# First attention layer: products read PSUM, the aggregate is no longer copied, VectorE's slots are dealt out anew

## The reference

```python
queries, gates = (qg[..., :DIM_KEYS], qg[..., DIM_KEYS:])
keys, values = (kv[..., :DIM_KEYS], kv[..., DIM_KEYS:])
queries, keys, values = (l2norm(queries), l2norm(keys), l2norm(values))
sim = jnp.einsum('bhid,bhjd->bhij', queries, keys)
attn = jnp.square(jax.nn.relu(sim))
aggr = jnp.einsum('bhij,bhjd->bhid', attn, values)
out = tanh_norm(aggr) * jnp.tanh(jax.nn.silu(gates))
return out.transpose(0, 2, 1, 3).reshape(b, n, h * d) @ Wout
```

## Time and profile before

| | us |
|---|---|
| median of 3 runs | 1835.48 |
| lowest, highest | 1835.18, 1840.15 |
| the profiled execution | 1857.31 |
| its span | 1854.6 |
| PE busy in the span | 1273.5 (69%) |
| DVE busy | 1229.5 (66%) |
| POOL busy | 926.3 (50%) |
| ACT busy | 740.7 (40%) |

### The profile page before, as it was taken

How to read it: one execution, slowest core, us unless ns; L and a number is a source line. 1 busy time by engine, 2 the same in 40 slices (tenths; PEclk the granted TensorE clock), 3 DMA queues, 4 the chain that set the end, 5 groups by cost and what they waited for, 6 DMA issues and landing times.

```text
span 1854.6 us, 27625 instructions
## 1 busy us (share of the span) xinstructions
PE 1273.5 (69%) x8554; PEld 857.2 (46%) x8555; DVE 1229.5 (66%) x2820; ACT 740.7 (40%) x1207; POOL 926.3 (50%) x996
## 2 busy tenths in 40 slices
PE   2434332548888887878788887568778777783775
PEld 1222221425666666656566667523333333331665
DVE  6778771157788887777777784266777677663443
ACT  1101100335455554455445544145555555552322
POOL 2355566546666666666666644321332313223663
PEclk8555555568888888888988886669988898986988
DMA  4000002600000000000000000030000000000110
GB/s 130 25 16 26 14 2 52 132 12 2 7 8 8 7 6 3 3 6 6 6 6 6 7 4 4 16 104 13 18 10 17 9 17 17 9 12 21 60 58 13
DMA packets 73493, 41.41 MB, mean 22 GB/s; under 512 B 23825, under 2 KB 68729, under 8 KB 73424
## 3 DMA queue, kind: packets, MB, share of 16 engines
q1 hardware_dynamic: 53040, 28.88, 5.6%
q0 software_dynamic: 20384, 11.67, 3.1%
HBM read 31.63 MB, written 23.87 MB: 30 GB/s over the span
## 4 chain that ended last, share of the span: by engine, by line
PE 40%; DVE 33%; issue 10%; ACT 6%; POOL 5%; DMA 2%; another core or an unknown queue 1%; POOLq 1%; DVEq 0%; SPq 0%; ACTq 0%
PE psum L1111 8%; PE psum L1162 5%; PE psum L1216 4%; DVE terms L1731 4%; DVE o L1573 4%; PE psum L1345 2%; PE psum L1358 2%; POOL o_inv L634 2%; PE psum L1139 2%; PE psum L1239 2%; PE psum L1249 2%; PE psum L1277 2%; PE psum L1120 1%; DVE rden L1425 1%; POOL xe_dram L573 1%
## 5 line engine op out<-in xcount | busy, mean ns | idle before, releaser
L1111 PE MATMUL psum<-v,attn 128*128 128x64 f32 x2048 | 288.5, 301 | 25.7 <-ACT aggr L845 17.1
L1111 PEld LDWEIGHTS psum<-v,attn 128*128 128x128 f32 x2048 | 272.7, 214 | 61.6 <-issue 44.9
L1731 DVE TENSOR_REDUCE terms<-psum 128x2 bf16<-128x512 f32 x256 | 165.5, 690 | 37.2 <-PE psum L1239 28.5
L609 POOL DMA_INDIRECT yg<-ye_dram,routel x128 | 139.2, 1088 | 65.5 <-issue 36.0
L695 POOL TENSOR_SCALAR veps<-meanvar 128x2 f32<-128x2 f32 x32 | 6.1, 191 | 330.9 <-DVE meanvar L1709 329.8
L573 POOL DMA_INDIRECT xe_dram<-rows_out,route x128 | 131.1, 1024 | 39.6 <-issue 38.7
L1216 PE MATMUL psum<-prob,v 128*32 128x256 f32 x1024 | 148.8, 415 | 1.1 <-ACT pvT L919 0.8
L914 ACT ACTIVATE prob<-psum 128x512 f32<-128x512 f32 x256 | 138.5, 597 | 18.8 <-PE psum L1204 18.8
L830 ACT ACTIVATE attn<-psum 128x1024 f32<-128x1024 f32 x128 | 129.9, 1015 | 11.9 <-PE psum L1094 10.7
L1120 PE MATMUL psum<-ident,o 128*128 128x128 f32 x256 | 48.5, 351 | 102.3 <-DVE o L1573 78.9
L1239 PE MATMUL psum<-k_highT,q_highT 32*128 32x256 bf16 x512 | 56.6, 303 | 76.9 <-DVE terms L1731 73.0
(11 more groups left out here) (297 smaller groups left out, 2975.8 us busy)
## 6 DMA issues: line engine op xcount, KB each, us to landing
x4n_dram<-x4n SPq DMA_DIRECT2D x16, 256.0 KB
w<-in_w POOLq DMA_DIRECT2D x48, 64.0 KB, 2.5
x_in<-in_x SPq DMA_DIRECT2D x8, 256.0 KB, 2.8
xe_dram<-zero_rows SPq DMA_DIRECT2D x8, 256.0 KB, 3.5
x_dram<-x1s SPq DMA_DIRECT2D x8, 256.0 KB
xe_dram<-rows_out,route POOLq DMA_INDIRECT x128
xe<-xe_dram SPq DMA_DIRECT2D x16, 128.0 KB
x1l<-x_dram SPq DMA_DIRECT2D x16, 128.0 KB, 2.2
```

The lines of the kernel that those rows point to most:

```text
L609: pool.indirect_dma_start(yg[p][:, j, k, :], None, ye_dram, bass.IndirectOffsetOnAxis(ap=where[:, j, K0 + k:K0 + k + 1], axis=0), bounds_c ...
L1111: mm = pe.matmul(psum[:, 4 + j, (head % HALF) * DV:(head % HALF + 1) * DV], attn[g % RING][:, h, c * SEQ + j * P:c * SEQ + (j + 1) * P], v ...
L1731: dve.tensor_reduce(terms4[:, 0, j, head:head + 2, 6, 0], bank[4 + a2].rearrange("q (b k) -> q b k", b=2), AX, ALU.max, negate=True).then_ ...
```

## The change

1. The aggregate is not copied. ACT squares banks 4 and 5 straight from PSUM in two pieces of 512 columns, and DVE multiplies the same banks with the unscaled gate (`product_with_gate`), also in two pieces, into `o`, of which there are now two tiles. ACT takes bank 4 first, DVE bank 5 first, then each waits for the other to be done with the second bank. PE may fill the banks again when both pieces of both engines are done.
2. POOL scales the product `o` with `o_factor` (`scale_output`) in place of the gate. There is no DVE instruction behind it: PE transposes each piece as soon as it is scaled.
3. The squares of the attention: DVE multiplies the relu in SBUF with the scores still in PSUM, now for six pairs; ACT squares pairs 2 and 4 in SBUF (`ACT_PAIRS`); POOL squares none. PE's `scores` of pair `g` waits for the square of pair `g-2` where DVE makes it.
4. On DVE, the product comes right behind the square in slots 1 and 5, `norm_of(tail, 1)` moves from slot 1 to the end of slot 2, the terms are split behind the product and the norm of slot 5, and combine is cut: two experts' rows in slot 4, two with the moments in slot 6; `normalise3` moves to slot 7.
5. On POOL, `length_of(att, 0)` comes behind `rstd3` instead of ahead of it.
6. On ACT, the first gate tanh moves from slot 5 to slot 4.

```diff
-        aggr = sb("aggr", [P, 2, 512])
-        o = sb("o", [P, 2, 512])
+        o = two("o", [P, 2, 512])
...
-        POOL_PAIRS = (2, 3, 6)
+        ACT_PAIRS = (2, 4)
+        DVE_PAIRS = tuple(g for g in range(PAIRS) if g not in ACT_PAIRS)
...
             def half(fetch, front, att, tail):
...
                 if tail:
                     length_of(tail, 1)
-                if att:
-                    square(att, POOL_PAIRS[0])
-                if tail:
-                    scale_gate(tail, 1)
-                if att:
-                    square(att, POOL_PAIRS[1])
+                    scale_output(tail, 1)
...
-                if att:
-                    length_of(att, 0)
                 if fetch:
                     hold(s["var3"], fetch.n)
...
                 if att:
-                    scale_gate(att, 0)
-                if att:
-                    square(att, POOL_PAIRS[2])
+                    length_of(att, 0)
+                    scale_output(att, 0)
...
             def take_aggregate(q, hf):
-                wait(act, s["o_made"], 2 * (q.n - 1) + hf)
+                wait(act, s["o_norm_made"], 2 * (q.n - 1) + hf)
                 act.wait_ge(s["attn_read"], PAIRS * (q.n - 1) + 4 * hf + 4)
-                act.activation(aggr[:], psum[:, 4:6, :], ACT.Copy).then_inc(s["aggr_out"], 1)
-                act.wait_ge(s["aggr_out"], 2 * (q.n - 1) + hf + 1)
-                act.activation(aggr_sq[:], aggr[:], ACT.Square).then_inc(s["aggr_sq_made"], 1)
+                act.activation(aggr_sq[:, 0, :], psum[:, 4, :], ACT.Square).then_inc(s["aggr_sq_made"], 1)
+                act.wait_ge(s["o_product"], 4 * (q.n - 1) + 2 * hf + 1)
+                act.activation(aggr_sq[:, 1, :], psum[:, 5, :], ACT.Square).then_inc(s["aggr_sq_made"], 1)
...
+                    if att and g in ACT_PAIRS:
+                        square(att, g)
+                    if front and g == 4:
+                        gate_tanh(front, 0)
...
             def scores(att, g):
-                wait(pe, s["relu_made"], PAIRS * (att.n - 1) + g - 1)
+                before, n = (g - 2) % PAIRS, att.n - 1 - (g < 2)
+                if before in ACT_PAIRS:
+                    wait(pe, s["relu_made"], PAIRS * n + before + 1)
+                else:
+                    wait(pe, s["attn_made"], len(DVE_PAIRS) * n + DVE_PAIRS.index(before) + 1)
...
                 if g % 4 == 0:
-                    wait(pe, s["aggr_out"], 2 * (q.n - 1) + hf)
+                    wait(pe, s["aggr_sq_made"], 4 * (q.n - 1) + 2 * hf)
+                    wait(pe, s["o_product"], 4 * (q.n - 1) + 2 * hf)
...
-                dve.tensor_tensor(r[:], r[:], r[:], ALU.mult).then_inc(s["attn_made"], 1)
+                dve.tensor_tensor(r[:], r[:], psum[:, 2 * (g % 2):2 * (g % 2) + 2, :], ALU.mult).then_inc(s["attn_made"], 1)
...
-            def gated_output(q, hf):
-                wait(dve, s["oT_ps"], 4 * (q.n - 1) + 2 * hf)
-                dve.wait_ge(s["gated"], 4 * (q.n - 1) + 2 * hf + 2)
-                dve.tensor_tensor(o[:], aggr[:], gate[q.p][:, :, 512 * hf:512 * hf + 512], ALU.mult).then_inc(s["o_made"], 1)
+            def product_with_gate(q, hf):
+                wait(dve, s["oT_ps"], 4 * (q.n - 2) + 2 * hf + 2)
+                dve.wait_ge(s["gate_made"], 2 * q.n)
+                dve.wait_ge(s["attn_read"], PAIRS * (q.n - 1) + 4 * hf + 4)
+                for j in (1, 0):
+                    if j == 0:
+                        dve.wait_ge(s["aggr_sq_made"], 4 * (q.n - 1) + 2 * hf + 1)
+                    dve.tensor_tensor(o[hf][:, j, :], psum[:, 4 + j, :], gate[q.p][:, j, 512 * hf:512 * hf + 512], ALU.mult).then_inc(s["o_product"], 1)
```

More of the change, by code:

```diff
@@ L837, in gate_tanh @@
             def gate_tanh(front, j):
[L838 removed]
+                wait(act, s["o_product"], 4 * (front.n - 2))
                 act.wait_ge(s["silu_made"], 4 * (front.n - 1) + 2 * j + 2)
@@ L887, in half @@
                         take_oT(tail, 1)
-                    if front and g == 5:
-                        gate_tanh(front, 0)
                     if att and g == 5:
@@ L1577, in take_oT, with combine @@
                 dve.tensor_copy(oT[:, 1, 4 * hf:4 * hf + 4, :], ring[OT_BANK[hf][1]][:].rearrange("q (c t) -> q c t", c=4)).then_inc(s["oT_dve"], 1)
-            def combine(front):
-                dve.wait_ge(s["x1l_landed"][front.p], 16 * front.k)
-                dve.wait_ge(s["yg_landed"][front.p], 16 * 2 * K0 * front.k)
-                for k in range(K0):
+            def combine(front, part):
+                if part == 0:
+                    dve.wait_ge(s["x1l_landed"][front.p], 16 * front.k)
+                    dve.wait_ge(s["yg_landed"][front.p], 16 * 2 * K0 * front.k)
+                for k in range(2 * part, 2 * part + 2):
                     for j in range(2):
@@ L1629, in half @@
                         square(tail, PAIRS - 1)
-                    if g > 0 and att and g - 1 not in POOL_PAIRS:
+                    if g > 0 and att and g - 1 in DVE_PAIRS:
                         square(att, g - 1)
@@ L1658, in half @@
                         v_sum(front, 3)
-                    if tail and g == 4:
-                        gated_output(tail, 1)
                     if front and g == 3:
```

62 lines of the change are left out of this document (33 added, 29 removed).

## The result

The changed kernel takes 1933.01 us (median of 4 runs, 1930.25 to 1944.54), the kernel before 1837.82 us (4 runs, 1835.18 to 1840.95). The ratio is 1.053, with a 95% interval from 1.048 to 1.058: 95 us slower. The forecast was 1917 us, with a range of 1868 to 1978.

A forecast was written before the change was run, and what follows sets the result against it. No engine is full; a 48 us step is PE work, low clock and idle. Per step -4.84 + 1.1 + 4.4 + 0.8 + 4.5 = +6.0 us, times 13.5 is 81 us: 1917 us, range 1868 to 1978.

The forecast's parts named there:

- The product leaves its place: DVE's gated product before the transposes of half 1: PE's wait of 4.84 us per step goes; pieces take 0.68 us.
- First cost: Turning of half 0: product pieces ahead of the value copies raise PE idle from 1.12 to about 2.2 us: +1.1.
- Second cost: Slot 2: ACT blocked at the tanh by the later norm; PE waits for the square of pair 2: +4.4.
- Third cost: Freeing the aggregate's banks: second pieces wait for the other engine's first, 2.0 us where one copy took 1.23: +0.8.
- Fourth cost: POOL's length of half 0 behind combine: PE's idle at the step's end goes from about 0.8 to 5.3 us: +4.5.
- The clock: PE's clock falls after the 4.4 us wait, losing 4.5 us as before at another place: net 0.
- rival B: PE's clock falls twice a step, each further fall 4.5 us: up to 1978 us, 1947 in half the steps; chance 0.20.
- Hidden: the multiply-adds: Combine's first part beside POOL's scaling of the values: multiply-adds taken as not held up, nothing charged.
- C: PE's clock stays up at the 4.4 us wait, saving about 3 us per step: 1876 us; chance 0.13.
- E: Effects cancel: second cost as reckoned, POOL's length early enough, no clock fall: about -20 to +20 us, 1835; chance 0.05.
- D: ACT reaches square of pair 2 within 4.3 us, neither stall nor clock fall: -8.2 per step, 1725 us; chance 0.06.

The follow-up runs named there:

- handover version: Changed kernel with norm in slot 1, length ahead of `rstd3`, DVE's slot 1 product behind the copies of values, ACT's slot 5 squares ahead of `oT`: 1762.27 us, 0.961.

## Why the prediction was right, and where it was not

**Direction and size.** Right. The profiled executions differ by 77 us, the sum said 81; the medians differ by 95. The 21.8 us by which the profiled execution of before lies over its median were carried over, and after's was not so far off its own: three of before's 13 steps are 50.5 to 51.1 us long and one 52.7, the others near 48, which is what I had taken as the step. Against that 48.0 the mean of after, 55.6, is +7.6 a step where +6.0 was forecast; against before's own mean of 49.0 it is +6.6. In 13.5 steps that makes 103 and 89 us, on either side of the 95 of the medians. So a step grew by 1 us or so more than forecast, and the terms make it up differently: that they sum to nearly the forecast is in part luck, as the terms below show.

**The product leaves its place (-4.84).** Confirmed. The wait is gone, the pieces take 0.69 us (0.68 by the earlier trace rows) and the squares from PSUM 1.21. Beside POOL's values stands a square, not the product as I had said: that begins 1.5 us after POOL is done (873.82, 867.95 + 4.40). It is the square that shows that an operand in PSUM keeps DVE clear of POOL.

**First cost (+1.1).** Confirmed to a tenth: 1.12 us became 2.16. With the product behind the copies it went back to 1.19.

**Second cost (+4.4).** Confirmed in place, releaser and mechanism: 4.0 us on average, 4.2 at most, with ACT in front of the tanh for 11.6 us (the 9 to 10 forecast was too short). What I had not seen is that PE's idle is not what makes up its price. Filling the idle with work that keeps the clock up, which leaves the wait, gave 15 us. Moving the tanh gave 88, more than that and the 54 us that 13.5 such waits contain. The tanh holds ACT, and behind ACT it holds DVE's inverse roots and with them all of the rest of the step. I had written that these stand behind the tanh, and then added up only PE's side of it.

**Third cost (+0.8).** Mechanism right, size wrong: 2.6 us on average where I took 2.0, before 1.23. ACT's first square (875.75) stands behind its copy `oT`, and DVE's second piece waits 1.88 us for it. That is +1.4 in place of +0.8.

**Fourth cost (+4.5).** The weakest term. The wait of ACT for the length came as forecast (10.43 us, forecast 10) and the second term transposes do wait for `qT`, but 2.45 us at most and 1.1 on average, not 2.9; the wait for `x3` of 0.9 did not appear; the last is 1.35 where 1.5 was reckoned. Together 2.5 against 5.3, so +1.7 in place of +4.5. The reckoning set PE's arrival with all rows at full clock. With a slower projection (5.30 us where I took 4.1), PE comes later and waits less. The run without this cost took 2.0 us off a step, near the 1.7.

**The clock (0).** Wrong, and the step of the forecast that failed; this is the part of rival B that came true. I had reckoned with one fall that only changes its place. In 5 of 13 steps there is another behind the longer idle in front of half 0's turning, in 11 of 13 the aggregate of pair 4 is slow again behind its wait (as it was in all 13 before, but there with the one fall at half 1's turning), and in 8 of 11 the queries' and keys' matmuls are slow behind the two waits that the fourth cost brings (in none of 13 before, and in none of 12 with the length first). By the stretches from 470 to 1090 us idle has grown by 2.7 a step (11.5 against 8.85; the terms above make 3.3), and PE's busy time, with the same matmuls, by 4.0 (44.1 against 40.1). The forecast had +6.0 and 0. So its sum was nearly right with much of the share turned round, and that is luck. Not all of the further low clock is on the path: the filling shows that most of what lies behind pair 2 is not.

**Hidden: the multiply-adds.** They are held, against my reading of the trace, and the rule that I set against it holds for POOL's long instructions. The Trainium skill (SBUF — State Buffer, "Who interferes with whom", practical consequences) says that a VectorE instruction with two SBUF inputs contends with a GpSimd instruction that reads SBUF. Beside POOL's scaling of the values this case agrees for multiply-adds (2.84 us for two, 0.35 each when moved), for squares (4.64) and for the scaling (4.00), and none with an operand in PSUM was held. The row that I took as counter-evidence had two multiply-adds beside `o_max` with 16 columns, which lasts 0.25 us and begins 0.27 us after them: there was nothing to wait for. But the six behind them do run beside POOL without being held. In the kernel before, 84 multiply-adds and 18 squares out of SBUF began while POOL's `o_inv` of 16 columns was under way, and took 0.34 to 0.35 us and 1.19 to 1.22 us each. So two SBUF inputs alone do not decide here; it matters which instruction POOL is at.

```profile
636.19 1.91 DVE L1586 SCALAR_TENSOR_TENSOR x<-yg,routel,x 128x128 f32<-128x128 f32 x6
```

```profile
636.15 2.93 POOL L634 TENSOR_TENSOR o_inv<-o_max,minus_half 128x16 f32<-128x16 f32 x1
```

The charge of nothing was right for the changed kernel, as the prediction says for both cases.

**What the sum left out.** In the kernel before, DVE's first three instructions of the inverse roots run beside POOL's scaling of the gate and its square. They have one SBUF input each and are held too: 0.65, 0.90 and 1.62 us on average from 470 to 1100 us. In the changed kernel POOL has no square there, and they take 0.92, 0.21 and 0.21. That shortens the chain from the tanh to the scores of pair 5 by 1.8 us a step, a gain that the sum has no term for. One of them in the kernel before, while POOL squares from 619.14 to 621.03:

```profile
619.28 1.82 DVE L1546 TENSOR_SCALAR inv<-guess 128x96 uint32<-128x96 uint32 x1
```

**The other rivals.** C (clock stays up) and E (cancel) are out by the low rows and the 2.4 us waits at the end. D is out for the changed kernel, but its condition, a tanh that comes 4.5 us earlier, is what the norm in slot 1 makes true: its single price of 1725 us was too good, since that run gives 1865, and with the length in its old place 1800.

## What to carry to other kernels

Before a small instruction is moved back in one engine's list, look for the wait that it feeds on another engine, and list everything that stands behind that wait: the price is that of the whole queue and of the engines fed by it, not the idle of the busiest engine in front of the first piece. The places of a norm (1.21 us) and a length (three POOL instructions, 3.4 us), both feeding a tanh of 0.22 us, decided here between +5.3% and -2.2%, with the heavy part of the change the same.

When two engines share out a buffer crosswise, put each one's first half ahead of any copy that nobody waits for yet; and when DVE works out of SBUF with two inputs, begin it before POOL's long operation and not behind it, or give it an operand in PSUM. The advice on the buffer rests on two moves that were made together (37 us), the advice on DVE and POOL on single edits (15 and 75 us).

## What the runs showed of the chip

**A short idle may or may not lower the clock.** In front of half 0's turning PE stood 1.11 to 1.20 us in each of 13 steps of the handover version and of the four built on it, and in 9 of 13 steps of the kernel before. The aggregate behind it took 2.0 us in all of those 74 cases. The four longer idles of the kernel before were followed by 3.67 us once (3.14 us of idle) and by 2.0 three times (2.58, 2.91 and 3.19). With 2.08 to 2.17 us of idle at the same place, in the same 13 steps, it took 3.2 to 3.7 us in 5 steps of the changed kernel, in 11 with the norm in slot 1, in 10 with the length first, in 8 with 16 matmuls put in, in 7 with the tanh in slot 4 and in 7 with norm and length, in 1 with the squares from SBUF and in none with 26 matmuls put in. And a shorter idle can do at another place: behind 1.63 to 1.76 us in front of the scores of pair 5, the turning of half 1 took 1.85 to 1.92 us in place of 1.04 in 9 of 13 steps of the handover version. So the length of the idle alone does not decide; what else does, no run here isolates.

**POOL is held up as well.** POOL's inverse root of 128x16 takes 2.94 us when nothing holds it (717.90 in the run with the square first); when DVE's terms with both inputs in SBUF had begun just ahead, it took 3.98. In the same step, POOL and the DVE row at that moment:

```profile
736.72 3.98 POOL L628 TENSOR_TENSOR o_inv<-o_max,minus_half 128x16 f32<-128x16 f32 x1
```

```profile
736.71 1.22 DVE L1624 TENSOR_TENSOR terms<-qk,terms 128x1024 f16<-128x1024 f32 x1
```

**So are POOL's gathers.** In the kernel before, an indirect transfer that POOL issues right behind the start of a DVE square out of SBUF took 2.01 us of POOL's time where the others take about 1.00:

```profile
602.66 2.01 POOL L609 DMA_INDIRECT yg<-ye_dram,routel  x1 [0.30 <-issue]
```

```profile
602.59 1.22 DVE L1563 TENSOR_TENSOR attn<-attn 128x1024 f32<-128x1024 f32 x1
```

I had not expected it. Two runs that differ only in the squares' operand show that the square is the cause. From 470 to 1100 us, with norm and length moved and the squares taking one operand from PSUM, none of 96 gathers took over 1.14 us; with both operands in SBUF, 13 of 96 took 1.31 to 2.02 us, and each of the 13 had been issued 0.08 to 0.78 us behind the start of such a square. In the kernel before it is 9 of 96, one of them behind a product out of SBUF.
